# One reciprocal of the product of two denominator halves, and ternary weight sums as two ScalarE passes

## What the reference computes

```
# conditioning (r = x, k = v = a side input, per channel and batch), c = 0..3
num = nf + nb - ekv + euk * v          # forward and backward decayed sums
den = df + db - ek + euk
base = sigmoid(x) * (num / maximum(den, 1e-8)) ; out = base * (0.8 + 0.2 tf)

# ternary weights of layer 0's feed-forward block, W1 (1024x256) and W2 (256x1024)
delta = 0.05 * max|W| ; mask = |W| > delta
n     = max(sum(mask), 1)
alpha = sum(|W| where mask) / n
W     = alpha * sign(W) * mask
```

## Time and profile before

| | |
|---|---|
| median of three runs | 920.1 us |
| the profiled execution's own time | 915.89 us |
| its span, first to last instruction | 914.1 us |
| VectorE (DVE) busy | 569.4 us, 62% |
| TensorE (PE) busy | 529.1 us, 58% |
| ScalarE (ACT) busy | 281.9 us, 31% |
| GpSimd (POOL) busy | 231.0 us, 25% |
| mean granted TensorE clock | 0.725 |

### The profile page before, as it was taken

How to read it: one execution, slowest core, us unless ns; L and a number is a source line. 1 busy time by engine, 2 the same in 40 slices (tenths; PEclk the granted TensorE clock), 3 DMA queues, 4 the chain that set the end, 5 groups by cost and what they waited for, 6 DMA issues and landing times. The chain is left out here.

```text
span 914.1 us, 17666 instructions
## 1 busy us (share of the span) xinstructions
PE 529.1 (58%) x7348; PEld 408.9 (45%) x7348; DVE 569.4 (62%) x1036; ACT 281.9 (31%) x710; POOL 231.0 (25%) x321
## 2 busy tenths in 40 slices
PE   0344741634656597446456536844786673399981
PEld 0233531523443243334344424633564563399981
DVE  6679489488895687675617652745264417377753
ACT  3331242133332451025640232323320304055520
POOL 2000000000000000200866812850285005324435
PEclk9766875676656799666567557965786955599996
DMA  8442050050001000461003400060000124466414
GB/s 319 130 96 36 1 104 0 1 104 0 1 1 47 1 0 0 99 142 41 3 4 70 79 7 4 20 128 8 6 10 6 12 110 174 165 220 216 142 39 135
DMA packets 52065, 61.28 MB, mean 67 GB/s; under 512 B 25408, under 2 KB 45392, under 8 KB 47504
## 3 DMA queue, kind: packets, MB, share of 16 engines
q1 hardware_dynamic: 50176, 55.15, 22.6%
q0 software_dynamic: 1808, 4.99, 1.8%
HBM read 45.24 MB, written 13.63 MB: 64 GB/s over the span
## 5 line engine op out<-in xcount | busy, mean ns | idle before, releaser
L749 PE MATMUL psum<-arena 128*32 128x32 bf16 (+20 forms) x5512 | 370.3, 281 | 283.3 <-DVE arena L1370 72.4
L749 PEld LDWEIGHTS psum<-arena 128*32 128x32 bf16 (+8 forms) x5512 | 269.0, 130 | 385.9 <-issue 84.9
L1804 POOL TENSOR_TENSOR arena<-arena 128x31 f32<-128x31 f32 (+15 forms) x124 | 69.3, 559 | 9.7
L1190 ACT ACTIVATE psum<-psum,arena 128x256 f32<-128x256 f32 (+7 forms) x128 | 45.7, 364 | 78.5 <-DVE arena L1431 78.5
L1802 POOL TENSOR_TENSOR arena<-arena 128x31 f32<-128x31 f32 (+15 forms) x124 | 64.6, 521 | 9.7
L1153 ACT ACTIVATE arena<-psum 128x512 f32<-128x512 f32 (+1 forms) x48 | 35.4, 737 | 62.5 <-PE psum L749 62.3
L1355 DVE RECIPROCAL arena<-arena 128x512 f32<-128x512 f32 x16 | 53.7, 3353 | 0.5
L1441 DVE TENSOR_REDUCE arena<-psum 128x2 f32<-128x512 f32 (+1 forms) x48 | 41.4, 862 | 19.5 <-PE psum L749 19.0
L1094 ACT ACTIVATE arena<-arena 128x255 f32<-128x255 f32 x64 | 27.1, 495 | 73.0 <-DVE arena L1333 73.0
L1347 DVE TENSOR_TENSOR_SCAN arena<-arena 128x255 f32<-128x255 f32 x64 | 42.6, 727 | 3.6 <-ACT arena L1094 3.4
L1815 POOL TENSOR_TENSOR fc_second_parts<-arena,fc_first_parts 128x2048 fp32r<-128x2048 f32 x6 | 27.9, 4652 | 63.5 <-ACT fc_first_parts L1258 63.5
(11 more groups left out here) (176 smaller groups left out, 955.9 us busy)
## 6 DMA issues: line engine op xcount, KB each, us to landing
arena<-fc SPq DMA_DIRECT2D x16, 1024.0 KB, 5.2
arena<-parts SPq DMA_DIRECT2D x40, 256.0 KB, 4.6
parts<-arena SPq DMA_DIRECT2D x16, 384.0 KB, 3.2
arena<-parts SPq DMA_DIRECT2D x40, 128.0 KB, 5.3
dispatched<-arena SPq DMA_DIRECT2D x1, 2048.0 KB, 16.9
arena<-arena SPq DMA_DIRECT2D x128, 8.0 KB
arena<-dispatched SPq DMA_DIRECT2D x8, 256.0 KB, 3.9
expert_rows<-arena SPq DMA_DIRECT2D x8, 256.0 KB, 2.2
```

Source lines behind the costliest of these rows:

```text
L749: return nc.tensor.matmul(out, lhsT, rhs, start=start, stop=stop)
L1190: ins = A(s_, s_, ACT.Exp, bias=nbias[:, n:n + 1], accum_out=ncc[b % 3][:, n:n + 1])
L1804: ins = G_.tensor_tensor(X3[:, k + 1:BLK, 0:w], X3[:, k + 1:BLK, 0:w], tmp, ALU.add)
```

## The change

Three edits go together. In `weigh`, the denominators' two halves (128 x 256 each) are multiplied, the reciprocal is taken of the product, and each half's reciprocal is that times the other half: the inner `[:, ::-1]` swaps the halves. In the ternary weights, the sum of the absolute values above the threshold is no longer taken from a product on VectorE: ScalarE computes the sums of Relu(W - delta) and Relu(-W - delta), and `alpha` adds delta times the count to their sum. The thresholds and these passes form a new step, `limit`, which stands in the list after `("weigh", 2, 0)` for W1 and after `("ternary", 0)` for W2; `first` is left as it was. The mask is written straight over the weights, in two passes.

```diff
--- before.py
+++ after.py
@@ -136,8 +136,8 @@
     o += groups("scores", 0, 0) + [("minus", 0, 0), ("max", 0, 0), ("weigh", 1, 0)]
 
     units = [[("wkv", 0, 3), ("scale", 0, 3), ("wkv", 1, 1), ("scale", 1, 1), ("weigh", 0, 3), ("weigh", 1, 1), ("wkv", 2, 0),
-              ("scale", 2, 0), ("largest", 0), ("largest", 1), ("weigh", 2, 0)],
-             [("wkv", 1, 2), ("scale", 1, 2), ("ternary", 0), ("weigh", 1, 2), ("wkv", 2, 1), ("scale", 2, 1), ("weigh", 2, 1)],
+              ("scale", 2, 0), ("largest", 0), ("largest", 1), ("weigh", 2, 0), ("limit", 0)],
+             [("wkv", 1, 2), ("scale", 1, 2), ("ternary", 0), ("limit", 1), ("weigh", 1, 2), ("wkv", 2, 1), ("scale", 2, 1), ("weigh", 2, 1)],
              [("wkv", 1, 3), ("scale", 1, 3), ("ternary", 1), ("weigh", 1, 3), ("wkv", 2, 2), ("scale", 2, 2), ("weigh", 2, 2)],
              [("wkv", 2, 3), ("scale", 2, 3), ("alpha", 0), ("alpha", 1), ("weigh", 2, 3)]]
     first = (4, 3, 3, 3)
@@ -454,6 +454,12 @@
         def tern_tmp(i):
             return v3(tern_flat, (CT, MT)[i])
 
+        def tern_part(i, k):
+            return small[:, 8 + 3 * i + k:9 + 3 * i + k]
+
+        def limit(i, k):
+            return small[:, 24 + 2 * i + k:25 + 2 * i + k]
+
         def x_count(g, b):
 
             return (g - 1) * B + b + 1
@@ -560,6 +566,8 @@
         tern_sum = sem("ternary_sums")
         tern_abs = sem("ternary_absolute")
         tern_cnt = sem("ternary_counts")
+        tern_lim = sem("ternary_limits")
+        tern_above = sem("ternary_excess_sums")
         w_first = sem("expert_weight_first_parts")
         w_second = [sem(f"expert_fc{i + 1}_second_parts") for i in range(2)]
         h_whole = sem("expert_hidden_activated")
@@ -1209,13 +1217,19 @@
                         prev = [s for s in ORDER if s[0] == "wo"][n - 1]
                         wait_pe(act, prev)
                     give_back(step, A(oT, v3(one(step[1], slot), CT), ACT.Copy))
+                elif kind == "limit":
+                    i = step[1]
+                    w_ = (w1, w2)[i]
+                    act.wait_ge(tern_lim, i + 1)
+                    if i:
+                        act.wait_ge(tern_abs, i)
+                    for k, sign in enumerate((1.0, -1.0)):
+                        A(tern_tmp(i), w_, ACT.Relu, bias=limit(i, 1), scale=sign, accum_out=tern_part(i, k)).then_inc(tern_above, 1)
+                        act.wait_ge(tern_above, 2 * i + k + 1)
                 elif kind == "ternary":
                     i = step[1]
-                    w_ = (w1, w2)[i]
-
-
                     act.wait_ge(tern_cnt, i + 1)
-                    A(tern_tmp(i), w_, ACT.Square, accum_out=small[:, 43 + 2 * i:44 + 2 * i]).then_inc(tern_abs, 1)
+                    A(tern_tmp(i), (w1, w2)[i], ACT.Square, accum_out=tern_part(i, 2)).then_inc(tern_abs, 1)
                 elif kind == "fc1":
                     _, h, m = step
                     slot = filled(step)
@@ -1352,14 +1366,16 @@
                     st(V.scalar_tensor_tensor(out=euk, in0=euk, scalar=EXP30, in1=fsT[:, :, bt(b)], op0=ALU.min,
                                               op1=ALU.mult))
                     link(V.tensor_scalar_max(scan[2], scan[2], 1e-8))
-                    st(V.reciprocal(scan[3], scan[2]))
+                    link(V.tensor_tensor(scan[3][:, 0], scan[2][:, 0], scan[2][:, 1], ALU.mult))
+                    st(V.reciprocal(scan[3][:, 1], scan[3][:, 0]))
                     link(V.tensor_tensor(scan[0], scan[0], euk, ALU.add))
+                    link(V.tensor_tensor(scan[1], scan[2][:, ::-1], scan[3][:, 1].unsqueeze(1).to_broadcast([P, CT, T]), ALU.mult))
                     if c == 2:
                         wait_pe(dve, ("proj", 0, b))
                     elif c == 3:
                         wait_pe(dve, ("fc1", b // 2, MT - 1))
                     V.scalar_tensor_tensor(out=G[c % 2][:, :, bt(b)], in0=scan[0], scalar=tf[:, 3 * B + b:3 * B + b + 1],
-                                           in1=scan[3], op0=ALU.mult, op1=ALU.mult).then_inc(gate_ready, 1)
+                                           in1=scan[1], op0=ALU.mult, op1=ALU.mult).then_inc(gate_ready, 1)
                     dve.wait_ge(gate_ready, n + 1)
                 elif kind == "gate":
 
@@ -1489,32 +1505,35 @@
                         dve.wait_ge(loaded["tern"], 32)
                     V.tensor_reduce(small[:, 32 + i:33 + i], (w1, w2)[i], axis=AX.XY, op=ALU.max,
                                     apply_absolute_value=True).then_inc(tern_in, 1)
+                elif kind == "limit":
+
+                    i = step[1]
+                    dve.wait_ge(tern_max, i + 1)
+                    st(V.tensor_scalar(limit(i, 0), small[:, 34 + i:35 + i], THRESHOLD, None, ALU.mult))
+                    V.tensor_scalar(limit(i, 1), small[:, 34 + i:35 + i], -THRESHOLD, None, ALU.mult).then_inc(tern_lim, 1)
+                    dve.wait_ge(tern_lim, i + 1)
                 elif kind == "ternary":
 
                     i = step[1]
                     w_ = (w1, w2)[i]
-                    s_ = small
-                    dve.wait_ge(tern_max, i + 1)
-                    st(V.tensor_scalar(s_[:, 36:37], s_[:, 34 + i:35 + i], THRESHOLD, None, ALU.mult))
-                    link(V.tensor_scalar(s_[:, 37:38], s_[:, 34 + i:35 + i], -THRESHOLD, None, ALU.mult))
                     tmp = tern_tmp(i)
-                    if i:
-                        dve.wait_ge(tern_abs, i)
-                    link(V.tensor_scalar(tmp, w_, s_[:, 36:37], None, ALU.is_gt))
-                    link(V.scalar_tensor_tensor(out=tmp, in0=w_, scalar=s_[:, 37:38], in1=tmp, op0=ALU.is_lt,
-                                                op1=ALU.subtract))
-                    link(V.scalar_tensor_tensor(out=w_, in0=w_, scalar=1.0, in1=tmp, op0=ALU.mult, op1=ALU.mult,
-                                                accum_out=s_[:, 42 + 2 * i:43 + 2 * i]))
-                    V.tensor_copy(w_, tmp).then_inc(tern_cnt, 1)
+                    settle()
+                    dve.wait_ge(tern_above, 2 * (i + 1))
+                    link(V.tensor_scalar(tmp, w_, limit(i, 1), None, ALU.is_lt))
+                    V.scalar_tensor_tensor(out=w_, in0=w_, scalar=limit(i, 0), in1=tmp, op0=ALU.is_gt, op1=ALU.subtract
+                                           ).then_inc(tern_cnt, 1)
                 elif kind == "alpha":
 
                     i = step[1]
                     s_ = small
                     dve.wait_ge(tern_sum, i + 1)
-                    link(V.tensor_scalar_max(s_[:, 48:49], s_[:, 47 + 4 * i:48 + 4 * i], 1.0))
-                    link(V.reciprocal(s_[:, 49:50], s_[:, 48:49]))
-                    V.tensor_tensor(s_[:, 56 + i:57 + i], s_[:, 46 + 4 * i:47 + 4 * i], s_[:, 49:50], ALU.mult
-                                    ).then_inc(tern_ready, 1)
+                    sums = s_[:, 16 + 3 * i:19 + 3 * i]
+                    st(V.tensor_scalar_max(s_[:, 48:49], sums[:, 2:3], 1.0))
+                    link(V.tensor_tensor(s_[:, 50:51], sums[:, 0:1], sums[:, 1:2], ALU.add))
+                    st(V.reciprocal(s_[:, 49:50], s_[:, 48:49]))
+                    link(V.scalar_tensor_tensor(out=s_[:, 51:52], in0=sums[:, 2:3], scalar=limit(i, 0), in1=s_[:, 50:51],
+                                                op0=ALU.mult, op1=ALU.add))
+                    V.tensor_tensor(s_[:, 56 + i:57 + i], s_[:, 51:52], s_[:, 49:50], ALU.mult).then_inc(tern_ready, 1)
                     dve.wait_ge(tern_ready, i + 1)
                 elif kind == "fc2":
                     _, h, c = step
@@ -1760,9 +1779,9 @@
                     pool.wait_ge(tern_max, i + 1)
                 elif kind == "ternary":
                     i = step[1]
-                    pool.wait_ge(tern_cnt, i + 1)
+                    pool.wait_ge(tern_above, 2 * (i + 1))
                     pool.wait_ge(tern_abs, i + 1)
-                    G_.partition_all_reduce(small[:, 46 + 4 * i:48 + 4 * i], small[:, 42 + 2 * i:44 + 2 * i], P, RED.add
+                    G_.partition_all_reduce(small[:, 16 + 3 * i:19 + 3 * i], small[:, 8 + 3 * i:11 + 3 * i], P, RED.add
                                             ).then_inc(tern_sum, 1)
                     pool.wait_ge(tern_sum, i + 1)
                 elif kind == "quant":
```

## The result

The changed kernel takes 920.58 us (median of 20 runs, 917.48 to 926.4), the kernel before 917.65 (20 runs, 907.82 to 922.76). The ratio is 1.0055, with a 95% interval of 1.0031 to 1.008: 5.0 us slower (2.8 to 7.3). The two medians alone differ by 2.9 us, but twenty executions of one kernel lie up to 15 us apart, so the interval says more than they do. The forecast's direction was right and its size (+7.8 us) on the high side; its time of 928 and its range from 923 up were wrong. The first three runs had put the kernel before at 920.1, twenty put it at 917.65, so 2.5 us of the miss of 7.3 are the base.

What follows compares the result with a forecast made beforehand. No engine is busy over 62%; waits bound the kernel, VectorE setting the pace between attention steps. Terms -2.9, -5.4, +8.0, +9.3 and -1.2 sum to +7.8 us on the median of 920.1: 928 us, range 923 to 932.5.

Steps and rivals of the forecast that it cites:

- seven weighings, to the end of (2,0): Layer 0 before 161.6 us: seven `weigh` steps on VectorE's path each save 0.41 us by the halved reciprocal, -2.9 us.
- W1's passes off VectorE: Before `otr` of batch 1: VectorE's product with sum, copy and thresholds leave, a gain of 3.7 us.
- order of batch 1, with (1,2) and (2,1): Batch 1: `limit` 1 displaces `weigh` (1,2) behind `wo` and gate, so VectorE loses its cover; +9.3 us before (2,1)'s -0.41.
- W2's passes, to `otr` of batch 2: Batch 2: the same 3.7 us leave VectorE, but TensorE's transposes end only at 245.80, so 1.7 us count.
- batch 3, "wo 2" to "wo 3": Between VectorE's `wo` of batches 2 and 3: VectorE waits there, so savings count nothing; 0 us.
- The weighings said to be hidden: Weighing (2,2), before a 4.22 us wait, and four of conditioning 3, beside 54 us of matmuls: they save nothing.
- (a): Batch 0: the wait of `limit` 0 has cover, so part 3 costs nothing; sum -0.2, time 920; chance 5%.
- (b): ScalarE: Relu needs a table, two loads for each `limit`, 5.1 us more, time 933; chance 4%.
- (d): In `weigh`: the pair trick gives nothing because the swapped product is dear; 4.5 us more, 932.4; chance 7%.
- Part 3: `limit` 0 in ScalarE's queue after `weigh` (2,0): exps wait behind two Relu passes, VectorE's scores come late; +8.0 us (+6.5 to +9.5).
- Rival (c): Behind 583 us: added rest raises TensorE's granted clock by a tenth, 13 us come back, 915, faster; chance 4%.
- a change of over 3 us in a stretch behind 366 us: Sign in the profile after: if a stretch behind 366 us changed its length by over 3 us, the prediction is wrong.

Runs made afterwards that it cites:

- pair alone: The kernel before with only the edit of `weigh` (reciprocal of the product), against the kernel before: ratio 0.9934 (0.9905 to 0.9963), 6.1 us faster.
- order alone: The kernel before, no ternary edit, with `weigh` (1,2) pushed behind `wo` and the gate of batch 1, against the kernel before: ratio 1.0039 (1.0004 to 1.0074).
- the control: The kernel before run again with no edit, against the kernel before: ratio 1.0002 (0.9969 to 1.0034).
- the repeated one: The changed kernel measured once more against the kernel before: ratio 1.0067 (1.0034 to 1.0099).

## Why the prediction was right or wrong

Point by point, from the profiled executions. The terms in the order of time, each the change of the distance between two marks:

| term | predicted | measured |
|---|---|---|
| seven weighings, to the end of (2,0) | -2.9 | -2.7 |
| `limit` 0 in ScalarE's queue | +8.0 | +6.9 |
| W1's passes off VectorE | -3.7 | -4.0 |
| order of batch 1, with (1,2) and (2,1) | +8.9 | +9.2 |
| W2's passes, to `otr` of batch 2 | -1.7 | -3.0 |
| weighing (1,3) | -0.4 | -0.4 |
| batch 3, "wo 2" to "wo 3" | 0 | -2.0 |
| weighing (2,3) | -0.4 | -0.4 |
| sum, at "long" | +7.8 | +3.6 |

**Right.** Both mechanisms, their places and nearly their prices. Undoing each moved its hole and no other, and undoing both turned a loss of 5 us into a gain of 11, where the terms that remain had promised 9.9. Of the 12.7 us at "long", though, 3.6 are the stage of batch 3, which the sum did not have. The price of the pair trick was right to a hundredth for one weighing. The weighings said to be hidden show no gain of their own: the stage of (2,2) less TensorE's busy time is 10.4 to 10.5 us with the trick (pair alone, changed) and without it (before, order alone), and in the first of conditioning 3 VectorE's wait for TensorE grew to 9.36 us from 8.77. Rivals (a), (b) and (d) did not occur: the scores came late, no load was added for Relu (four before and four after; the Trainium skill, "ScalarE: Activation LUTs", section "Table sets: the hidden batching unit", has relu in every set, and the trace agrees), and the pair trick brings its 0.41 us.

**Right by chance.** The term of -2.7. The gains of the first four weighings were all but lost on the way. The projections of batch 0 began 0.41 us earlier and ended 0.08 later, and by 104.05 only 0.13 us was left; TensorE in the changed kernel:

```profile
23.24 8.23 PE L757 MATMUL psum<-arena 128*128 128x256 f32 x24 [23.24 <-DVE arena L1386]
47.55 9.16 PE L757 MATMUL psum<-arena 128*128 128x256 f32 x40 [16.09 <-DVE arena L1386]
...
104.05 9.90 PE L757 MATMUL psum<-arena 128*128 128x256 f32 x88 [1.61 <-DVE arena L1386]
```

The stretch at 104.05 then took 9.90 us where the same 88 matmuls had taken 11.23 before, at a granted clock of 0.83 in place of 0.73, and that paid it back. The expectation for the pair alone puts the losses of the first two stretches down to a lower clock. Of the first that is not so: it took 8.23 us in place of 7.74 at a granted clock of 1.00 in both profiles, and why stays open.

**Wrong: every TensorE stretch was taken at the length it had before.** This is the step that failed. Part 3 was set against scores groups that follow as slowly as before: the hole itself was 8.6 us (158.91 to 167.51), but 1.6 came back within the stage (161.65 to 173.32 before, 167.51 to 177.55 after, 11.7 against 10.0 us). What was left, 6.9, still lies inside that part's own bound (+6.5). The next two had no bound. The 1.7 of W2 was capped by transposes at 244.71, which came sooner with shorter scores and a shorter `pv` (4.53 us), so that 3.0 counted. Batch 3, "it waits instead", was put at nothing, and became 2.0 shorter. Rival (c) named the clock but looked for it only behind 583 us and priced it as one piece of over 10 us. It came in pieces of 1 to 2, in four stages of layer 0 (in the one of `limit` 0 together with shorter waits). The range had no room for the 3.3 us of W2 and batch 3, and its bottom, 923, stood on a base that was 2.5 us high. With the base of 917.65 the sum would have said 925.4; with the terms measured in layer 0 as well, 921.3, against 920.58.

**Open.** The rest behind "long" was 612.4 and 612.2 us in the two profiles of the change, 607.5 and 611.5 in those of before, and 607.7 to 610.7 in the other kernels of the table of marks. The prediction named a change of over 3 us in a stretch behind 366 us as a sign that it was wrong; it is there (4.7 us behind the 120 matmuls), but the control's rest moved by 4.0 without any change. By the ratios, the first comparison (5.0 us) leaves 1.4 us beyond the 3.6 of layer 0 and the repeated one (6.2 us) 2.6; by the medians it is -0.7 and 1.1. Whether the change shifts layer 1 into a slower position, or this is chance, four profiles don't tell.

## What to carry to other kernels

A step in a list that all engines walk has a price in every queue it enters: before pricing its instructions, ask what stands behind it on the engine that has to wait. Here the wait for two thresholds, and the Relu passes of 4 us behind it, held up ready exps for 16 (ScalarE was free at 147.5 and began them at 163.45). Where an order is cut by position (`units[b][first:first + 1]`), an inserted element moves its neighbours, and the work moved may have been the cover for something else. And the same passes cost next to nothing (0.3 us) in a gap where both engines already wait; look for that gap before giving up an offload.

## What the runs showed of the hardware

The same stage, with the same TensorE instructions and the same pauses between them, took TensorE 17.95 us or 15.95 at a granted clock of 0.56 or 0.64, each value in both profiles of its kernel (within 0.03 us), and adding 3.4 us of work ahead of it made it 1.0 us shorter in all. I had expected such stretches to keep their length. The runs show that they do not when something ahead of them shifts, and that two executions of one kernel agree in this stage; whether the moment or the rests ahead decide, they do not show. The Trainium skill, "TensorE: Matmul & The Clock Gate", section "Part 1: The HAM clock gate (the "warmup" mystery)", says that the chip's count of activity runs freely, and is not started by the kernel's own matmuls; no run here shows that count itself, and two executions of one kernel came out alike. So a saving ahead of TensorE work can be lost, or grow, by 1 to 3.6 us in one stage (28.4 us before, 26.4 and 24.8 in others), and a difference of that size needs marks and a control, not one span.

A Relu with a bias per partition over 2048 columns took 2.00 us, the Square without one 1.91.
